# The corrections of clipped states in the mixer: a sorted list of places, worked four at a time, instead of a walk over all rows

## Chip, cores, metric

One core of a Trainium2 chip runs a whole model of four layers in one program. The metric is the device time of one execution in microseconds. The kernel before took 3464.84 us (median of 3 runs, 3463.93 to 3465.86).

## The reference, cut to what matters

The first half of layer 0 is a mixer over 4 sequences of 1024 steps with 128 channels. It widens the 128 channels to 256 and runs 16 states for each of them, forward and backward in time:

```
h0 = 0
step:  h = clip(h * A + x_t * Bm, -10, 10)      # A, Bm: 256 x 16
       y = sum over the 16 states of h * C      # C: 256 x 16
out = (forward + backward) * 0.5 * silu(gate);  result = out @ out_proj_w
```

A is -clip(exp(A_log), -10, -0.01), and because exp(A_log) is positive that is 0.01 for every state. Without the clipping, each state is therefore its Bm times one common scan of x. The clipping matters only where that product leaves the range -10 to 10. A top-2 mixture of 8 experts (128 to 256 to 128) over the same tokens follows in the same stage, and six more parts of the model after it.

## The kernel before, in words

All that the change touches is in `mixer_and_top2`, the first stage. Channels lie on the 128 partitions. A row k (0 to 3) is one of two directions times one of two channel tiles, and `S[k]` is its plain scan over 1024 steps, with 32 zero columns ahead of it (`LEAD`), since a correction begins 32 steps early. For sequence b, VectorE does this, in the order that its program writes out at the end of the function:

- `scan` (L618) makes S for the four rows. `reaches` (L622 to L624) takes the largest |S| of every 256 steps (`CHUNK`) and multiplies it by |B| of every state: 128 x 256 numbers (4 rows, 4 places, 16 states).
- `gains` writes G, the output as if no state were clipped. `take_masks` (L634 to L649) compares `most` with 9.99 on one partition and leaves, for each (row, state), the number and the place of 256-step pieces in which a state can be clipped: a mask of those with one such piece, a mask of those with several, and the places.
- `corrections` walks the masks twice, first those with one piece, then those with several (`many`). A walk is a loop over the 4 rows; each pass loads the row's mask into a register (L675), tests each group of four states, and in a group that has any, each state. A state that is set is worked by `correct` (L595 to L611): it loads the place into a register, writes 2 x 288 limits (L605, L606), scans 576 elements (L608), and adds 256 of the results to G (L611). Both arms of every test add the same numbers to the semaphore `fix`, so `gated` (L688 on) can wait for a constant.
- `gated` writes y = (G forward + G backward) * gate (L692, L693). TensorE's output product of the sequence (L312) waits for y; everything of that sequence's experts comes behind it.

The order over the sequences: for sequence 0 nothing is there to lie beside the corrections. For sequences 1 to 3, TensorE, ScalarE and GpSimd run the experts of the sequence before; TensorE's program has `output(p)` at a fixed place among them (turn 9 of 35, `MIXED`), and GpSimd's has `largest(p + 2)` at turn 20 (`REACH`), between products `weigh` (L560) for which TensorE's L352 waits. VectorE's `route` and `normalise` for the sequence before are ahead of `take_masks` in its own order.

Of the kernel before, what the change touches and what calls it, by code (L numbers as in the profile page):

```python
# [143 lines left out]
def mixer_and_top2(nc, X, XN, XT, ident, x_dram, in_proj_w, A_log, B_mat, C_mat, out_proj_w, ln_w, ln_b, gate_w, gate_b, w1, b1, w2, b2):  # L144
# [13 lines left out]
    QUAD = 4  # L158
# [6 lines left out]
    LEAD, CHUNK = 32, 256  # L165
    NCHUNK = SEQ // CHUNK
    WINDOW, ROW = LEAD + CHUNK, LEAD + SEQ
    LAG = 3
# [19 lines left out]
    with Stage(nc, "mix") as s:  # L188
# [5 lines left out]
        limS, nCBS = (s.sb(n, [P, NSEG, DS]) for n in ("limS", "nCBS"))  # L194
# [6 lines left out]
        S = s.sb("S", [P, NSEG, ROW])  # L201
        G = s.sb("G", [P, NSEG, SEQ])
        S_flat, G_flat = S[:].rearrange("p k t -> p (k t)"), G[:].rearrange("p k t -> p (k t)")
# [3 lines left out]
        bit = s.sb("bit", [1, NSEG, DS])  # L207
        place = s.sb("place", [1, NSEG, NCHUNK, DS])
        flags, placed = (s.sb(n, [1, NSEG, NCHUNK, DS]) for n in ("flags", "placed"))
        count, place_f, one, many = (s.sb(n, [1, NSEG, DS]) for n in ("count", "place_f", "one", "many"))  # L210
        mask_f = s.sb("mask_f", [1, 2, NSEG])
        masks = s.sb("masks", [1, 2, NSEG], mybir.dt.int32)
        places = s.sb("places", [1, NSEG * DS], mybir.dt.int32)
# [26 lines left out]
        fix = [s.sem(f"fix{b}") for b in range(BATCH)]  # L240
# [11 lines left out]
        with nc.Block() as block:  # L252
# [299 lines left out]
            def _(pool):  # L552
# [18 lines left out]

                largest(0)
# [14 lines left out]
            def _(dve):  # L587
# [3 lines left out]
                def correct(b, k, d, many):  # L591
                    n = k * DS + d
                    done = (many * NSEG * DS + n) * 3
                    if many:
                        steps, lead = SEQ, 0  # L595
                        sk = S_flat[:, bass.ds(k * ROW + LEAD, SEQ)]
                        gk = G_flat[:, bass.ds(k * SEQ, SEQ)]
                    else:
                        steps, lead = WINDOW, LEAD
                        at = dve.value_load(places[0:1, bass.ds(n, 1)], min_val=0, max_val=SEQ - CHUNK)  # L600
                        sk = S_flat[:, bass.ds(k * ROW + at, WINDOW)]
                        gk = G_flat[:, bass.ds(k * SEQ + at, CHUNK)]
                    L = limS[:].rearrange("p k d -> p (k d)")[:, bass.ds(n, 1)]
                    w = nCBS[:].rearrange("p k d -> p (k d)")[:, bass.ds(n, 1)]
                    ts(d1[:, 0:steps, 0], sk, -1.0, L, ALU.mult, ALU.add)  # L605
                    ts(d1[:, 0:steps, 1], sk, L, None, ALU.add).then_inc(fix[b], 1)  # L606
                    dve.wait_ge(fix[b], done + 1)
                    nc.vector.tensor_tensor_scan(q[:, 0:steps].rearrange("p t a -> p (t a)"), d0[:, 0:steps].rearrange("p t a -> p (t a)"),  # L608
                                                 d1[:, 0:steps].rearrange("p t a -> p (t a)"), 0.0, ALU.mult, ALU.min).then_inc(fix[b], 1)
                    dve.wait_ge(fix[b], done + 2)  # L610
                    stt(gk, q[:, lead:steps, 1], w, gk, ALU.mult, ALU.add).then_inc(fix[b], 1)  # L611
# [16 lines left out]
                def gains(b):  # L628
                    for k in range(NSEG):
                        c.link(ts(G[:, k], S[:, k, LEAD:], gain[:, k % CT:k % CT + 1], None, ALU.mult))  # L630

                def take_masks(b):
                    dve.wait_ge(most_ready, b + 1)
                    c.link(ts(flags[:], most[0:1].rearrange("p (s c d) -> p s c d", c=NCHUNK, d=DS), BOUND * 0.999, None, ALU.is_gt))  # L634
                    tt(placed[:], flags[:], place[:], ALU.mult).then_inc(ch, 1)
# [2581 lines left out]
```

## Time and profile before

| | |
|---|---|
| three runs | 3463.93, 3465.86, 3464.84 us |
| the profiled execution | 3498.89 us, span 3497.2 us, mean granted clock 0.883 |
| TensorE busy | 79% |
| VectorE busy | 54% |
| ScalarE, GpSimd busy | 40%, 27% |
| mixer stage with the top-2 experts | 0 to about 570 us |
| sequence 0: VectorE from the end of its list to y | 46.9 to 186.9 us |

Durations are of the profiled execution, which is 34 us longer than the median of the runs. "Idle before" in brackets is the time the engine sat idle ahead of an instruction, with what ended it; "issue" means that it waited for nothing the profile shows, and "DVEq" is VectorE's own sequencer, which for these lines is the register work and branches of the walk. Register, branch and semaphore instructions are not counted as busy and have no rows.

### The profile page before, as it was taken

The page shows a single profiled execution, that of the slowest core. Times are in us where ns is not written, and L with a number is a line of the kernel's source. Part 1 is how long each engine was busy: PE and PEld are TensorE (multiplying, and loading weights), DVE is VectorE, ACT ScalarE, POOL GpSimd, SP SyncE. Part 2 cuts the span into 40 slices and gives each one's busy share as a digit, 9 for nine tenths or more (in the row PEclk, how much of TensorE's full clock was granted, in tenths as well). Part 3 has the DMA queues.
Part 4 walks back from the last instruction along what each step waited for, and adds up shares of the span by engine and source line. Part 5 has one row for each costly group of instructions (what it writes and reads, how often), then busy time and mean ns, then how long its engine had stood idle before and what let it go on. Part 6 is the DMA issues. An engine that isn't in the chain of part 4 may idle for free. (4 is left out here: it accounts for less than half of the span.)

```text
span 3497.2 us, 32456 instructions
## 1 busy us (share of the span) xinstructions
PE 2779.8 (79%) x10134; PEld 1389.7 (40%) x10146; DVE 1899.3 (54%) x3672; ACT 1407.3 (40%) x2163; POOL 936.7 (27%) x606
## 2 busy tenths in 40 slices
PE   2047888999999979999978777595799999659517
PEld 1023444555555544444444443243233333137503
DVE  6546532222222276656455458312777777489786
ACT  1023433111111146666644421133477877526403
POOL 0014563000000000000033320303499999600005
PEclk6568999999999989999968888897899999779658
DMA  2011121000000066665500012011000000100001
GB/s 54 0 31 40 49 58 37 0 0 0 0 0 0 0 146 145 144 140 141 120 5 1 0 43 57 31 43 51 25 1 1 10 1 1 33 2 1 1 0 31
DMA packets 107458, 126.08 MB, mean 36 GB/s; under 512 B 22283, under 2 KB 60300, under 8 KB 107052
## 3 DMA queue, kind: packets, MB, share of 16 engines
q1 hardware_dynamic: 105260, 120.13, 14.1%
q0 software_dynamic: 2048, 4.20, 0.4%
q8 instruction: 64, 1.05, 0.1%
q14 instruction: 86, 0.70, 0.1%
HBM read 108.55 MB, written 14.16 MB: 35 GB/s over the span
## 5 line engine op out<-in xcount | busy, mean ns | idle before, releaser
L2432 PE MATMUL dots_x<-all_xt,delta_wE 128*128 128x512 f32 x768 | 366.2, 613 | 3.7 <-DVE dots_g L2527 2.3
L2417 POOL TENSOR_TENSOR dots_pr<-dots_g 128x512 f32<-128x512 f32 (+2 forms) x96 | 305.6, 3204 | 56.1 <-DVE dots_g L2527 48.2
L971 DVE SCALAR_TENSOR_TENSOR attn_sim<-attn_sc,attn_mask 128x512 f32<-128x512 f32 (+3 forms) x256 | 125.8, 491 | 316.9 <-PE attn_sc L897 313.8
L897 PE MATMUL attn_sc<-attn_q,attn_xb 128*128 128x512 f32 (+3 forms) x768 | 295.0, 486 | 0.0
L908 PE MATMUL attn_op<-attn_sim,attn_v 128*128 128x512 f32 (+3 forms) x768 | 295.0, 486 | 0.0
L1257 DVE TENSOR_TENSOR grp_h<-grp_sq,grp_cb 128x512 f32<-128x512 f32 x256 | 176.7, 692 | 191.1 <-ACT grp_sq L1145 170.7
L1085 PE MATMUL grp_po<-grp_h,grp_down 128*128 128x512 f32 x512 | 266.1, 602 | 6.1 <-DVE grp_h L1257 6.1
L1077 PE MATMUL grp_ph<-all_xt,grp_up 128*128 128x512 f32 x512 | 264.0, 598 | 0.5 <-ACT grp_sg L1161 0.5
L2524 DVE TENSOR_TENSOR dots_m<-dots_x,dots_sg 128x512 f32<-128x512 f32 x256 | 173.9, 689 | 137.3 <-PE dots_x L2432 131.1
L1139 ACT ACTIVATE grp_r<-grp_ph 128x512 f32<-128x512 f32 x272 | 162.4, 597 | 185.4 <-PE grp_ph L1077 183.7
L2432 PEld LDWEIGHTS dots_x<-all_xt,delta_wE 128*128 128x128 f32 x768 | 135.9, 190 | 234.8 <-issue 139.3
L560 POOL TENSOR_TENSOR mix_h<-mix_r,mix_cb 128x512 f32<-128x512 f32 x128 | 172.1, 1352 | 151.3 <-ACT mix_r L474 117.2
L2417 POOL TENSOR_TENSOR all_xn<-dots_g 128x1536 f32<-128x1536 f32 (+2 forms) x64 | 205.2, 3223 | 11.0 <-DVE dots_g L2527 5.6
L897 PEld LDWEIGHTS attn_sc<-attn_q,attn_xb 128*128 128x128 f32 x768 | 141.0, 190 | 125.7 <-issue 107.1
L908 PEld LDWEIGHTS attn_op<-attn_sim,attn_v 128*128 128x128 f32 x768 | 141.0, 190 | 98.4 <-issue 68.9
L2527 DVE SCALAR_TENSOR_TENSOR dots_g<-dots_m,dots_x 128x512 f32<-128x512 f32 x256 | 163.1, 679 | 0.0
L946 ACT ACTIVATE attn_sim<-attn_sc 128x512 f32<-128x512 f32 x128 | 76.4, 597 | 205.6 <-PE attn_sc L897 205.6
L1145 ACT ACTIVATE grp_sq<-grp_r 128x512 f32<-128x512 f32 x256 | 159.1, 621 | 0.0
L474 ACT ACTIVATE mix_r<-mix_ph,mix_b1s 128x512 f32<-128x512 f32 x128 | 87.9, 687 | 160.2 <-PE mix_ph L344 137.1
L1085 PEld LDWEIGHTS grp_po<-grp_h,grp_down 128*128 128x128 f32 x512 | 94.6, 191 | 138.7 <-issue 95.9
L352 PE MATMUL mix_acc<-mix_h,mix_w2s 128*128 128x512 f32 x256 | 132.2, 606 | 20.4 <-POOL mix_h L560 20.4
L312 PE MATMUL mix_po<-mix_woT,mix_y 128*128 128x128 f32 x128 | 20.1, 331 | 157.8 <-DVE mix_y L693 157.8
(622 smaller groups left out, 4947.2 us busy)
## 6 DMA issues: line engine op xcount, KB each, us to landing
grp_cb<-grp_combine SPq DMA_DIRECT2D x512, 128.0 KB, 3.3
mix_cb<-top_weights SPq DMA_DIRECT2D x64, 256.0 KB, 3.2
cap_xs<-cap_zero SPq DMA_DIRECT2D x7, 320.0 KB, 5.0
experts_xe<-cap_xs SPq DMA_DIRECT2D x7, 320.0 KB, 3.2
all_x<-in_L_attn_x_dram SPq DMA_DIRECT2D x4, 512.0 KB, 5.3
cap_w<-in_L_ffn_W_dram SPq DMA_DIRECT2D x1, 2048.0 KB, 8.9
cap_ys<-experts_yo SPq DMA_DIRECT2D x8, 256.0 KB, 2.3
delta_h<-all_xn SPq DMA_DIRECT2D x1, 2048.0 KB
```

Of the source, the lines that this page charges most:

```text
L560: nc.gpsimd.tensor_tensor(h[:, J % HB], r[:, J % RB], cb[:, n % CB], ALU.mult).then_inc(h_ready, 1)
L897: nc.tensor.matmul(sc[k % SC][:, 0:w], xb[:, m * P:(m + 1) * P], q[:, par, n0:n0 + w], start=True, stop=True).then_inc(s_mm, 1)
L908: ins = nc.tensor.matmul(op[half][:, n0 - half * GROUP:n0 - half * GROUP + w], v[:, par, m], sim[:, par, k, 0:w], start=False, stop=False)
L1077: nc.tensor.matmul(ph[J % 2][:], w, XT[:, g * GROUP:(g + 1) * GROUP], start=True, stop=True).then_inc(up_mm, 1)
L1085: nc.tensor.matmul(po[g % 2][:], w, h[:, J % HB], start=(j == 0), stop=(j == NJ - 1)).then_inc(down_mm, 1)
L1139: nc.scalar.activation(r[:, J % RB], ph[J % 2][:], ACT.Relu).then_inc(relu_done, 1)
L1145: nc.scalar.activation(sq[:, J % RB], r[:, J % RB], ACT.Square).then_inc(sq_done, 1)
L1257: tt(h[:, J % HB], sq[:, J % RB], cb[:, n % CB], ALU.mult).then_inc(h_done, 1)
L2417: nc.gpsimd.tensor_tensor(slot[w % SLOTS][:, at:at + n], a_, b_, ALU.mult).then_inc(pool_ready, 1)
L2432: nc.tensor.matmul(bank(n, sh)[:], wE[:, 1 - k % 2, a, sh], XTj[:, k // 2, par::2], start=True, stop=True).then_inc(u_mm, 1)
L2524: tt(m[:, n % 2, sh - 1], bank(n, sh)[:], sg[:, n % 2], ALU.mult).then_inc(m_ready, 1)
L2527: ins = stt(g[:, I % 2, sh - 1, k], m[:, n % 2, sh - 1], 0.0, bank(n, 0)[:], ALU.max, ALU.mult)
```

## The change

Places are 128 steps long instead of 256, so a window is 160 columns and `reach` and `most` have 512 columns instead of 256. `take_masks` makes one number for every (row, state) that has just one place: `found` holds the place, `first_code` the row and the state, and together they are column * 128 + (row * 16 + state + 1). Eight rounds of top-eight and replace sort the 64 numbers in descending order. What has several places goes into masks as before, with their sum ahead of them. `corrections` goes over 4 parties of 16 entries of the sorted list. Where the first of a party is not zero, it works four times four entries: four register loads, then for each entry the addition of the result of the group before (`add_pending`) and its two limit instructions, and at the end one scan over 4 x 160 x 2 elements. Empty entries within a party work on a limit of 1 and a weight of 0. The last four results are added after the loop. The walk over rows with several places is behind one test of the sum. G gets rows of 1056 columns, so that one offset serves S and G. GpSimd makes the constant tables. In all:

```diff
-    LEAD, CHUNK = 32, 256
+    LEAD, CHUNK = 32, 128
+    ENTRIES = NSEG * DS
+    RADIX = 128
+    STEP = CHUNK * RADIX
+    SINGLE, SEVERAL = NCHUNK * STEP, 2 * NCHUNK * STEP
...
     (GpSimd, before largest(0))
+                for c_ in range(NCHUNK):
+                    nc.gpsimd.memset(place[:, :, c_], float(SINGLE + c_ * STEP))
+                for d in range(DS):
+                    nc.gpsimd.memset(bit[:, :, d:d + 1], float(1 << d))
+                    for k in range(NSEG):
+                        last = nc.gpsimd.memset(first_code[:, k, d:d + 1], float(k * ROW * RADIX + k * DS + d + 1))
+                last.then_inc(tables, 1)
+                nc.gpsimd.memset(q[:, 2 * CT * C // 2:SEQ // 2], 0.0).then_inc(tables, 1)
...
+                def none_pending():
+                    for i in range(QUAD):
+                        dve.reg_mov(last_at[i], 0)
+                        dve.reg_mov(last_col[i], 0)
+
+                def add_pending(b, i):
+                    at = dve.snap(last_at[i], min_val=0, max_val=(NSEG - 1) * ROW + SEQ - CHUNK)
+                    col = dve.snap(last_col[i], min_val=0, max_val=ENTRIES)
+                    gk = G_flat[:, bass.ds(at, CHUNK)]
+                    stt(gk, q[:, i * WINDOW + LEAD:(i + 1) * WINDOW, 1], nCBS[:, bass.ds(col, 1)], gk, ALU.mult, ALU.add).then_inc(bounded[b], 1)
+
+                def correct_four(b, n):
+                    code = [dve.value_load(codes[0:1, bass.ds(n * QUAD + i, 1)], min_val=0, max_val=LAST_CODE) for i in range(QUAD)]
+                    dve.wait_ge(traced[b], n + 1)
+                    for i in range(QUAD):
+                        if i:
+                            dve.wait_ge(bounded[b], n * (QUAD + 1) + i)
+                        add_pending(b, i)
+                        at, col = code[i] >> 7, code[i] & (RADIX - 1)
+                        dve.reg_mov(last_at[i], at)
+                        dve.reg_mov(last_col[i], col)
+                        sk, L = S_flat[:, bass.ds(at, WINDOW)], limS[:, bass.ds(col, 1)]
+                        ts(d1[:, i * WINDOW:(i + 1) * WINDOW, 0], sk, -1.0, L, ALU.mult, ALU.add)
+                        last = ts(d1[:, i * WINDOW:(i + 1) * WINDOW, 1], sk, L, None, ALU.add)
+                    last.then_inc(bounded[b], 1)
+                    dve.wait_ge(bounded[b], (n + 1) * (QUAD + 1))
+                    nc.vector.tensor_tensor_scan(q[:, 0:QUAD * WINDOW] ..., d0[:, 0:QUAD * WINDOW] ...,
+                                                 d1[:, 0:QUAD * WINDOW] ..., 0.0, ALU.mult, ALU.min).then_inc(traced[b], 1)
...
     (correct becomes correct_row: the same four instructions over 1024 steps, for rows with several places)
...
                 def take_masks(b):
                     dve.wait_ge(most_ready, b + 1)
-                    (thresholds, count, places, two masks: 10 instructions)
+                    c.link(stt(flags[:], most[0:1] ..., BOUND * 0.999, place[:], ALU.is_gt, ALU.mult))
+                    c.link(redu(total[:], flags[:].rearrange("p s c d -> p s d c"), AX.X, ALU.add))
+                    (several, found; mask_f, begin; mask_f sum, left: three pairs on 1 x 64; masks)
+                    for i in range(ENTRIES // EIGHT):
+                        top = listed[:, i * EIGHT:(i + 1) * EIGHT]
+                        c.link(nc.vector.max(top, left[:, i % 2]))
+                        if i + 1 < ENTRIES // EIGHT:
+                            c.link(nc.vector.match_replace(left[:, (i + 1) % 2], top, left[:, i % 2], 0.0))
+                    c.link(ts(listed[:], listed[:], float(SINGLE), 0.0, ALU.subtract, ALU.max))
+                    c.link(nc.vector.tensor_copy(codes[:], listed[:]))
...
                 def corrections(b):
                     dve.sem_inc(apart, 1)
-                    for many in range(2):
+                    dve.sem_inc(traced[b], 1)
+                    none_pending()
+                    with dve.Fori(0, ENTRIES // PARTY) as party:
+                        leader = dve.value_load(codes[0:1, bass.ds(party * PARTY, 1)], min_val=0, max_val=LAST_CODE)
+                        with dve.If(leader > 0):
+                            with dve.Fori(0, PARTY // QUAD) as four:
+                                correct_four(b, party * (PARTY // QUAD) + four)
+                            dve.sem_inc(apart, 1)
+                        with dve.Else():
+                            dve.sem_inc(traced[b], PARTY // QUAD)
+                            dve.sem_inc(bounded[b], (QUAD + 1) * (PARTY // QUAD))
+                    dve.wait_ge(traced[b], ENTRIES // QUAD + 1)
+                    for i in range(QUAD):
+                        add_pending(b, i)
+                        dve.wait_ge(bounded[b], ENTRIES // QUAD * (QUAD + 1) + i + 1)
+                    any_row = dve.value_load(masks[0:1, 0:1], min_val=0, max_val=NSEG * (2 ** DS - 1))
+                    with dve.If(any_row > 0):
                         with dve.Fori(0, NSEG) as k:
                             (as before, with correct_row)
+                    with dve.Else():
+                        dve.sem_inc(fix[b], 3 * ENTRIES)
```

## Rows read from the trace of the kernel before

**Rows 1.** Stages: window, length, busy of five engines with instructions, granted clock, DMA share, GB/s.
```profile
47.00:187.00 140.00, 6.51 (x8) 2.44 (x8) 70.03 (x113) 2.65 (x5) 0.00 (x0) 0.51 0.00 0
```

**Rows 2.** Waits of TensorE, 185 to 560 us: who for whom, total, times, longest.
```profile
PE mix_po L312 <- DVE mix_y L693: 157.8, 3, 138.0
PE mix_acc L352 <- POOL mix_h L560: 20.4, 2, 10.3
```

**Rows 3.** Timeline of VectorE, list making of sequence 0: start, duration, instruction, idle before.
```profile
44.17 0.27 DVE L634 TENSOR_SCALAR mix_flags<-mix_most 1x256 f32<-1x256 f32 x1
...
44.82 0.56 DVE L636 TENSOR_REDUCE mix_count<-mix_flags 1x64 f32<-1x256 f32 x1
...
46.75 0.16 DVE L649 CAST mix_masks<-mix_mask_f 1x8 int32<-1x8 f32 x1
49.48 0.37 DVE L605 TENSOR_SCALAR mix_d<-mix_S,mix_limS 128x288 f32 x1 [2.56 <-issue]
```

**Rows 4.** Timeline of VectorE, corrections of sequence 0 and one scan after.
```profile
79.08 0.37 DVE L605 TENSOR_SCALAR mix_d<-mix_S,mix_limS 128x288 f32 x1 [1.22 <-issue]
...
82.70 0.37 DVE L605 TENSOR_SCALAR mix_d<-mix_S,mix_limS 128x288 f32 x1 [0.85 <-issue]
...
95.56 0.37 DVE L605 TENSOR_SCALAR mix_d<-mix_S,mix_limS 128x288 f32 x1 [2.38 <-issue]
...
186.88 1.22 DVE L692 TENSOR_TENSOR mix_y<-mix_G 128x1024 f32<-128x1024 f32 x1 [13.00 <-DVEq L686]
...
202.36 2.29 DVE L618 TENSOR_TENSOR_SCAN mix_S<-mix_decay,mix_xs 128x1024 f32<-128x1024 f32 x1
```

**Rows 5.** Groups by line, 0 to 700 us: a correction's instructions; busy, mean ns.
```profile
L608 DVE TENSOR_TENSOR_SCAN mix_q<-mix_d 128x576 f32<-128x576 f32 x28 | 38.0, 1358 | 1.0
...
L611 DVE SCALAR_TENSOR_TENSOR mix_G<-mix_q,mix_nCBS,mix_G 128x256 f32 x28 | 13.6, 485 | 6.7 <-DVE mix_q L608 6.7
...
L605 DVE TENSOR_SCALAR mix_d<-mix_S,mix_limS 128x288 f32 x28 | 10.4, 371 | 49.3 <-issue 49.3
```

**Rows 6.** Groups by line, whole run: VectorE's top-eight and replace instructions.
```profile
L3057 DVE MATCH_REPLACE8 sink_left<-sink_best,sink_left 32x1024 f32<-32x1024 f32 x15 | 17.9, 1196 | 0.0
...
L1224 DVE MAX8 grp_top<-grp_v 128x8 f32<-128x64 f32 x32 | 4.8, 213 | 0.0
...
L3057 DVE MATCH_VALUE_LOAD sink_left<-sink_best,sink_left 32x8 f32 x15 | 1.2, 79 | 0.5
```

**Rows 7.** Timeline of VectorE: first instruction behind the walks of sequences 1, 2, 3.
```profile
264.30 1.23 DVE L692 TENSOR_TENSOR mix_y<-mix_G 128x1024 f32<-128x1024 f32 x1 [28.76 <-DVEq L686]
...
349.65 1.22 DVE L692 TENSOR_TENSOR mix_y<-mix_G 128x1024 f32<-128x1024 f32 x1 [19.52 <-DVEq L686]
...
437.97 1.34 DVE L692 TENSOR_TENSOR mix_y<-mix_G 128x1024 f32<-128x1024 f32 x1 [29.16 <-DVEq L686]
```

**Rows 8.** Timeline of GpSimd around its all-reduces.
```profile
41.63 1.20 POOL L570 PARTITION_ALL_REDUCE mix_most<-mix_reach  x1 [39.83 <-issue]
215.03 1.06 POOL L570 PARTITION_ALL_REDUCE mix_most<-mix_reach  x1 [172.20 <-DVE mix_reach L624]
...
312.92 1.08 POOL L570 PARTITION_ALL_REDUCE mix_most<-mix_reach  x1 [6.01 <-issue]
321.12 4.92 POOL L560 TENSOR_TENSOR mix_h<-mix_r,mix_cb 128x512 f32<-128x512 f32 x4 [7.12 <-issue]
```

**Rows 9.** Timeline of TensorE: output products of sequences 1, 2, 3.
```profile
269.35 6.51 PE L312 MATMUL mix_po<-mix_woT,mix_y 128*128 128x128 f32 x32 [17.67 <-DVE mix_y L693]
...
360.00 3.73 PE L312 MATMUL mix_po<-mix_woT,mix_y 128*128 128x128 f32 x32
...
445.98 3.84 PE L312 MATMUL mix_po<-mix_woT,mix_y 128*128 128x128 f32 x32 [2.14 <-DVE mix_y L693]
```

**Rows 10.** DMA queues, 60 to 173 us: packets, MB, share of the 16 engines.
```profile
q14 instruction: 1, 0.01, 0.0%
```

**Rows 11.** The same, 235.6 to 264.3 us.
```profile
q14 instruction: 5, 0.04, 0.4%
```

More of the change, by code:

```diff
@@ L206, in mixer_and_top2 @@
         most = s.sb("most", [P, NSEG * NCHUNK * DS])
[L207 to L213, printed above, removed]
+        bit, first_code, several = (s.sb(n, [1, NSEG, DS]) for n in ("bit", "first_code", "several"))
+        place, flags = (s.sb(n, [1, NSEG, NCHUNK, DS]) for n in ("place", "flags"))
+        total, found, begin = (s.sb(n, [1, NSEG, DS]) for n in ("total", "found", "begin"))
+        left = s.sb("left", [1, 2, ENTRIES])
+        listed = s.sb("listed", [1, ENTRIES])
+        mask_f = s.sb("mask_f", [1, 1 + NSEG])
+        masks = s.sb("masks", [1, 1 + NSEG], mybir.dt.int32)
+        codes = s.sb("codes", [1, ENTRIES], mybir.dt.int32)
         gw = s.sb("gw", [P, E])
@@ L239, in mixer_and_top2 @@
             "reach_ready", "most_ready", "out_mm", "x_added", "vector_chain", "apart"))
-        fix = [s.sem(f"fix{b}") for b in range(BATCH)]
+        fix, bounded, traced = ([s.sem(f"{n}{b}") for b in range(BATCH)] for n in ("fix", "bounded", "traced"))
+        tables = s.sem("tables")
         gates_in, w1_in, w2_in, stats_done, var_ready, std_ready, xn_ready = (s.sem(n) for n in (
@@ L589, in _ @@
                 tt, ts, stt, redu = nc.vector.tensor_tensor, nc.vector.tensor_scalar, nc.vector.scalar_tensor_tensor, nc.vector.tensor_reduce
-                def correct(b, k, d, many):
-                    n = k * DS + d
[L593 to L606, printed above, removed]
+                last_at = [nc.alloc_register(mybir.EngineType.DVE, f"last_at{i}") for i in range(QUAD)]
@@ new lines, in _ @@
+                last_col = [nc.alloc_register(mybir.EngineType.DVE, f"last_col{i}") for i in range(QUAD)]
+                def none_pending():
[7 more added lines that the diff above has]
+                    stt(gk, q[:, i * WINDOW + LEAD:(i + 1) * WINDOW, 1], nCBS[:, bass.ds(col, 1)], gk, ALU.mult, ALU.add).then_inc(bounded[b], 1)
@@ L629, in gains @@
                     for k in range(NSEG):
-                        c.link(ts(G[:, k], S[:, k, LEAD:], gain[:, k % CT:k % CT + 1], None, ALU.mult))
+                        c.link(ts(G[:, k, 0:SEQ], S[:, k, LEAD:], gain[:, k % CT:k % CT + 1], None, ALU.mult))
                 def take_masks(b):
                     dve.wait_ge(most_ready, b + 1)
-                    c.link(ts(flags[:], most[0:1].rearrange("p (s c d) -> p s c d", c=NCHUNK, d=DS), BOUND * 0.999, None, ALU.is_gt))
-                    tt(placed[:], flags[:], place[:], ALU.mult).then_inc(ch, 1)
@@ L636, in take_masks @@
-                    redu(count[:], flags[:].rearrange("p s c d -> p s d c"), AX.X, ALU.add).then_inc(ch, 1)
+                    if b == 0:
+                        dve.wait_ge(tables, 2)
+                    c.link(stt(flags[:], most[0:1].rearrange("p (s c d) -> p s c d", c=NCHUNK, d=DS), BOUND * 0.999, place[:], ALU.is_gt, ALU.mult))
+                    c.link(redu(total[:], flags[:].rearrange("p s c d -> p s d c"), AX.X, ALU.add))
+                    stt(several[:], total[:], float(SEVERAL), bit[:], ALU.is_ge, ALU.mult).then_inc(ch, 1)
@@ L640, in take_masks @@
[L640 to L642 removed]
+                    redu(mask_f[:, 0:1], mask_f[:, 1:], AX.X, ALU.add).then_inc(ch, 1)
+                    tt(left[:, 0].rearrange("p (s d) -> p s d", d=DS), found[:], begin[:], ALU.add).then_inc(ch, 1)
+                    c.n += 2
                     dve.wait_ge(ch, c.base + c.n)
[L644 removed]
@@ L746, in _ @@
                 c.link(nc.vector.memset(S[:, :, 0:LEAD], 0.0))
-                for c_ in range(NCHUNK):
-                    last = nc.vector.memset(place[:, :, c_], float(c_ * CHUNK))
-                c.link(last)
                 c.link(stt(nCB[:], Cm[:], -0.5, B[:], ALU.mult, ALU.mult))
```

63 lines of the change are left out of this document (36 added, 27 removed).

## The prediction

> **What bounds the kernel now.** I read the 40 slices of the page first: TensorE is at 70 to 100% nearly everywhere, but at 20, 0 and 40% in the first three slices of 87 us. The stage table shows why: in the 140 us from 47 to 187 us TensorE works 6.5 us at a granted clock of 0.51, GpSimd not at all, and VectorE 70 us [rows 1]. TensorE's waits name it: of 157.8 us waited for the mixer's y, 138.0 are one wait, that of sequence 0 [rows 2]. All of VectorE's corrections lie on the path there. The timeline of VectorE then shows that all 28 corrections of the run belong to sequence 0 [rows 5], and that the walks of sequences 1 to 3 find nothing and still take 28.8, 19.5 and 29.2 us [rows 7]. The third is as long as the first; the second is shorter because its sequencer had run ahead while VectorE was held up in the instructions before. Of these, TensorE waits 17.7 us for sequence 1, nothing for sequence 2 and 2.1 us for sequence 3 [rows 9].
>
> **What the data ask for.** I computed the plain scans and reaches from the reference's inputs: 28 (row, state) pairs of sequence 0 pass 9.99, as in the trace, and none of the other sequences. Each of the 28 lies in a single piece, with 256 and with 128 steps alike. So the new list has 28 entries: two parties run, eight groups of four with four blank entries in the last, and the walk over rows is skipped in all four sequences.
>
> **What a register instruction costs.** Within a group of states, the next state follows after 0.85 us idle if it is set and 1.22 us if one is skipped [rows 4]. A skip is four sequencer instructions, so 0.092 us each. Between the addition and the next limits are eight sequencer instructions with one load: 0.85 + 0.485 for the addition that they run beside [rows 5], so 1.34 us, less seven of 0.092: a load from SBUF is about 0.6; I take 0.55. An empty pass of 22 is then 21 x 0.092 + 0.55 = 2.5 us; the second walk of sequence 0 took 13.00 us for four [rows 4], 3 us more. Eight are 20 us against 28.8 [rows 7], 9 more, with five packets of instruction code in that stretch [rows 11], so a missing block of code costs some 1.8 us (the queue is shared by several engines: an estimate).
>
> **Part 1, the corrections of sequence 0.** Before: from the end of the list, 46.9 [rows 3], to 186.88 [rows 4], 140.0 us: four instructions of 0.37, 0.37, 1.36 and 0.485 a correction [rows 5], about 2.77 with their overlap, x 28 = 78, the rest sequencer.
> After, one group of four. VectorE: elements cost 1.02 ns (top-eight of 64 in 0.213, replace of 1024 in 1.196 [rows 6]), so the limits take 0.371 - 0.131 = 0.24 and the addition 0.35; the scan's slope is (2.29 - 1.36) / 448 = 2.08 ns [rows 4, 5], so 1280 elements take 2.82. Sum 8 x 0.24 + 4 x 0.35 + 2.82 = 6.1 us. Sequencer: I count 4 x 4 instructions for the loads, 4 x 13 for the entries (two snapped registers with their checks, addresses, waits on register values, shift and mask), five for scan and loop: 73 with 4 loads, 69 x 0.092 + 4 x 0.55 = 8.5 us. The loads, 3.3 us, can run while the previous scan is at work; the rest, 5.2, covers limits and additions, and at its end the last limits and the start of the scan cost 0.2 more: 8.7 us. No row shows a load beside a long scan. Bounds: VectorE alone, 6.1, and nothing beside anything, 8.5 + 6.1 = 14.6. The nearest rows, where sequencer work does run beside the addition, speak for the middle; I take 8.7. Eight groups: 70 us (49 to 117).
> Around them: 12 instructions ahead (1.1), four passes of the party loop (ten with a load, 1.4 us each, 5.6), the tail of four additions each waited for (36 instructions, 3.3, plus 0.5), the test with its load (1.1), three missing blocks of code (5.4; the jump over the 250 instructions of the row walk is one): 17 us. Together 87 against 140.0: -53. What it hides: nothing else was running, so the whole of it counts, and what is late next at y is VectorE itself.
>
> **Part 2, making the list.** Before: 44.17 to 46.9, 2.7 us [rows 3]. After: the first instruction 0.485 + 0.26 = 0.75 over 512 columns, the reduction 0.56 + 0.26 = 0.82 [rows 3, 5], five short steps on 64 columns 1.3, eight top-eights at 0.213 + 0.04 for the chained wait, seven replaces at 0.079 + 0.21 + 0.04 [rows 6], two at the end 0.45: 7.6 us, +4.9. The reach takes 0.3 more. On the path for sequences 0 and 1.
> The all-reduce has twice the columns. For sequence 0 the library load is behind the wait for reach, so it is at work from 41.63 [rows 8] and done by 44.17, where VectorE goes on without waiting [rows 3]: 1.2 to 2.5 us, which doubled ends at 44.0 to 46.7. I put 1 us on it (0 to 2.5).
> Sequence 0 so far: -53 + 4.9 + 0.3 + 1 = -46.8.
>
> **Part 3, sequences 1 to 3.** The empty walk becomes 12 + 4 x 10 + 36 + 7 = 95 instructions with 5 loads, 11.0 us, + 0.5 for additions that can't hide, + three missing blocks 5.4: 17 us (11 to 22). Sequence 1: -11.8 + 5.2 = -6.6, of the 17.67 us that TensorE waits [rows 9]; all of it counts. Sequence 2: TensorE came to its product without a wait [rows 9], since the four instructions that make y, from 349.65 on [rows 7] and 1.2 to 2.2 us each, had ended 3.5 us before; the walk's gain (2.5) less 5.2 eats 2.7 of these: 0. Sequence 3: y comes 7 us earlier, of which 2.1 count [rows 9].
> The all-reduces of sequences 2 and 3 sit in GpSimd's queue between products: 6.0 + 1.1 + 7.1 = 14 us each from product to product, with TensorE waiting 10.3 and 10.1 [rows 2, 8]. Each grows by 1.1 (its recorded length) to 2.2 us, and TensorE waits for it: +3.3. The 89 small memsets on GpSimd and the one of 128 x 256 x 2 lie in its idle 39.8 us at the start [rows 8]; uncovered they would cost at most some 9 us. VectorE's own memsets that go (0.6 us) lay ahead of a wait for ScalarE.
> Sum: -46.8 - 6.6 - 2.1 + 3.3 = -52 us: 3498.9 to 3447 for the profiled execution. The median of the runs is 34 us below; nothing in the stage depends on what makes that difference, so 3464.8 - 52 = 3413.
>
> **A page weighed.** In 113 us of sequence 0's loop, with its 302 instructions, one packet of code came [rows 10]; in the 29 us of a first pass over new code, five [rows 11]. The Trainium skill (Runtime: NRT & Kernel Launch, Instruction fetch mechanics) says that a taken branch whose target isn't in the current two pages of 256 instructions forces a fetch. By that rule a body of 302 could be fetched anew with each of four passes, which rows 10 don't show; the new inner body, some 75, would stay. The rule speaks for the jump over the row walk, priced above as a missing block.
>
> **Rivals.**
> A. Register loads wait until VectorE is idle, so nothing lies beside the scan: 11.5 us a group, +22: 3435. For: the 1.34 us above also fit a load that waited for the addition. Chance 0.17.
> B. Register work is cheaper than counted, several operations being packed into one instruction, and a group takes 7 us: -14, and 2 less for each walk: 3397. For: the packing is seen in the kernel before. Chance 0.15.
> C. The walks of sequences 1 to 3 don't shrink, because jumps over code make new misses (28 us stay): sequence 1 costs +5.2 instead of -6.6, sequence 3 +3 instead of -2.1, sequence 2 +1.7: 3432. Against: 95 instructions in place of 176. Chance 0.1.
> D. Slower than before: each pass of the loop over four fetches its code anew, because the body, the party's head and the walk behind them share blocks. From 15.2 us a group on, the change loses: 14.6 with nothing overlapped and one fetch of 1.8 is 16.4, x 8 = 131 against 70: +61, 3474. Against: rows 10. Chance 0.03.
> E. It doesn't do what it says: a single entry counted as several places opens the row walk. Four passes of 3.25 us, and limits, scan and addition over 1024 steps at the slopes above, 8.9 us: +22, 3435. Against: the inputs. Chance 0.02.
> The forecast keeps 0.53.
>
> **How the numbers follow.** Predicted 3413. A range of 3388 to 3440 takes in the forecast with a group at 7.5 to 10, rivals A, C and E, and the near part of B; outside are the far part of B and D. Of this kernel 0.2% (7 us) is about what can be told from no change. Faster: all but D and what lies near it, 0.96; within 0.2%: 0.01; slower 0.03.
>
> **What would show it.** In the new profile: y of sequence 0 at 137 to 142 us; eight scans of 128 x 1280 of 2.8 us each, spaced 8.7 us (11.5: A; 7: B; over 15: D); 7.6 us from the first instruction of the list to its end; a gap behind the walks of sequence 1 of 17 us or less (28: C); TensorE's wait for y of sequence 0 near 91 us and of sequence 1 near 11, none for 3; GpSimd's pauses at the all-reduces 15 to 16 us. No scan of 2048 elements (E). The forecast is wrong if the scans' spacing is off by more than 3 us, or if TensorE's wait for sequence 0 shrinks and a later wait, for y of 2 or for GpSimd, grows by as much.

## The result, and the profile after

The changed kernel takes 3381.47 us (median of 4 runs, 3380.22 to 3382.33) against 3465.35 us for the kernel before on the same chip: a ratio of 0.9759, 95% interval 0.9744 to 0.9773, or -84 us. The forecast was -52, in the range 3388 to 3440. The direction was right, the size was not.

The profiled execution of the changed kernel took 3380.9 us. The one of before took 3498.9 us, 34 us more than the runs. Later runs of the kernel before, on three chips, took 3497 to 3498 us on two of them and 3462 us on the third, so this profile most likely comes from a chip of the slower kind. The two kinds differ by some 36 us in one place, between the first write of the capacity routing's zeroed tables (2106.3 in the profile of before, 2026.0 after) and the first sums of the delta rule (2502.0 and 2385.2): 395.7 against 359.2 us. That stretch is the same code, and its length goes with the chip and not with the kernel: it is 394 to 397 us in all nine profiles of the slower kind, seven of them of other kernels than before, and 359 to 360 us in all five of the faster. Everything below is about the mixer stage, which ends with the first weight copy of the attention behind it: 590.8 us before, 512.2 after, -78.6 us. Second profiles of the two kernels have 593.7 and 513.4, so a difference of stages is known to some 3 us.

The stage that was nearly empty is about half as long. The stage table of the changed kernel (columns as in [rows 1]) shows its first 69 us, with VectorE busy for 53 of them; y begins 3.6 us later, so that like for like, from 47 us to y, it is 72.6 us in place of 139.9:

```profile
47.00:116.00 69.00, 6.68 (x12) 2.57 (x10) 53.03 (x140) 3.17 (x5) 0.00 (x0) 0.52 0.00 0
```

TensorE's waits in the changed kernel, 110 to 480 us, answer to [rows 2]: 138.0 has become 70.1, only one other wait for y is left (2.0 us), and there is a new row, 7.3 us for the normalised input of sequence 2.

```profile
PE mix_po L320 <- DVE mix_y L764: 72.1, 2, 70.1
PE mix_acc L360 <- POOL mix_h L568: 22.7, 5, 11.3
...
PE mix_tr L329 <- DVE all_xn L718: 7.3, 1, 7.3
```

The timeline of VectorE in sequence 0 answers to [rows 3, 4]: first and last instruction of the list, start of the first group, scans of the first groups, the passage from the first party to the second (81.72 to 86.75), the last scan, the first addition of the tail and the first instruction of y.

```profile
45.44 0.67 DVE L676 SCALAR_TENSOR_TENSOR mix_flags<-mix_most,mix_place 1x512 f32<-1x512 f32 x1
...
52.78 0.18 DVE L698 CAST mix_codes<-mix_listed 1x64 int32<-1x64 f32 x1
58.31 0.35 DVE L619 SCALAR_TENSOR_TENSOR mix_G<-mix_q,mix_nCBS,mix_G 128x128 f32 x1 [5.35 <-issue]
...
61.42 2.83 DVE L636 TENSOR_TENSOR_SCAN mix_q<-mix_d 128x1280 f32<-128x1280 f32 x1
65.15 0.35 DVE L619 SCALAR_TENSOR_TENSOR mix_G<-mix_q,mix_nCBS,mix_G 128x128 f32 x1 [0.90 <-DVE mix_q L636]
...
68.23 2.83 DVE L636 TENSOR_TENSOR_SCAN mix_q<-mix_d 128x1280 f32<-128x1280 f32 x1
...
81.72 2.83 DVE L636 TENSOR_TENSOR_SCAN mix_q<-mix_d 128x1280 f32<-128x1280 f32 x1
86.75 0.35 DVE L619 SCALAR_TENSOR_TENSOR mix_G<-mix_q,mix_nCBS,mix_G 128x128 f32 x1 [2.21 <-issue]
...
110.05 2.83 DVE L636 TENSOR_TENSOR_SCAN mix_q<-mix_d 128x1280 f32<-128x1280 f32 x1
114.01 0.35 DVE L619 SCALAR_TENSOR_TENSOR mix_G<-mix_q,mix_nCBS,mix_G 128x128 f32 x1 [1.13 <-DVEq L732]
...
119.64 1.23 DVE L763 TENSOR_TENSOR mix_y<-mix_G 128x1024 f32<-128x1024 f32 x1 [3.71 <-DVEq L757]
```

The list takes 7.5 us, 45.44 to 52.96. The scans start 6.8 us apart, once 8.1 where the party changes. Between a scan's end (64.25) and the next addition (65.15) there are 0.90 us, in the later groups 0.82 to 0.84.

Sequence 1 in the same timeline, for [rows 7]: the last instruction ahead of the walk ends at 173.47. The first of the four blank additions is at 177.78 and y begins at 184.11. The empty walk with its additions takes 10.6 us, where it took 28.8.

```profile
177.78 0.35 DVE L619 SCALAR_TENSOR_TENSOR mix_G<-mix_q,mix_nCBS,mix_G 128x128 f32 x1 [4.31 <-DVEq L732]
...
184.11 1.22 DVE L763 TENSOR_TENSOR mix_y<-mix_G 128x1024 f32<-128x1024 f32 x1 [3.65 <-DVEq L757]
```

The code packets in that stretch (the queue view, columns as in [rows 11]), two where there were five:

```profile
q14 instruction: 2, 0.02, 0.4%
```

TensorE's timeline, for [rows 9]: the output products of sequences 0 to 3, and the turning of the normalised input ahead of the second.

```profile
124.70 5.59 PE L320 MATMUL mix_po<-mix_woT,mix_y 128*128 128x128 f32 x32 [70.06 <-DVE mix_y L764]
...
172.59 1.08 PE L329 MATMUL mix_tr<-all_ident,all_xn 128*128 128x128 f32 x4 [7.34 <-DVE all_xn L718]
...
192.01 5.47 PE L320 MATMUL mix_po<-mix_woT,mix_y 128*128 128x128 f32 x32 [2.00 <-DVE mix_y L764]
...
281.93 3.73 PE L320 MATMUL mix_po<-mix_woT,mix_y 128*128 128x128 f32 x32
...
367.97 3.73 PE L320 MATMUL mix_po<-mix_woT,mix_y 128*128 128x128 f32 x32
```

GpSimd's timeline, for [rows 8]: the all-reduce with 512 columns is recorded with 1.80 us instead of 1.08, and the two pauses between products go from 14.2 and 14.0 us to 14.8 and 15.2.

```profile
234.36 1.80 POOL L578 PARTITION_ALL_REDUCE mix_most<-mix_reach  x1 [5.84 <-issue]
243.28 4.92 POOL L568 TENSOR_TENSOR mix_h<-mix_r,mix_cb 128x512 f32<-128x512 f32 x4 [7.12 <-issue]
```

From these rows comes the ledger of the stage:

| stretch | before | after | change | forecast |
|---|---|---|---|---|
| to the first output product | 191.9 | 124.7 | -67.2 | -46.8 |
| first to second | 77.4 | 67.3 | -10.1 | -6.6 |
| second to third | 90.7 | 89.9 | -0.7 | +1.65 |
| third to fourth | 86.0 | 86.0 | +0.1 | -0.45 |
| fourth to the attention | 144.8 | 144.2 | -0.6 | 0 |

### The profile page after: what moved, and what is told of

Its sections match the earlier page's. It is cut to its first block and busy times, and to the rows that moved or that the text cites. A ratio compares the mean times of both kernels' runs of the same rounds, so it can differ in the third digit from the quotient of the medians.

```text
span 3379.1 us, 32162 instructions
## 1 busy us (share of the span) xinstructions
PE 2774.0 (82%) x10146; PEld 1388.3 (41%) x10146; DVE 1909.5 (57%) x3754; ACT 1408.2 (42%) x2163; POOL 946.8 (28%) x695
## 3 DMA queue, kind: packets, MB, share of 16 engines
q0 software_dynamic: 2048, 4.20, 0.4%
## 5 line engine op out<-in xcount | busy, mean ns | idle before, releaser
L2484 POOL TENSOR_TENSOR all_xn<-dots_g 128x1536 f32<-128x1536 f32 (+2 forms) x64 | 205.2, 3224 | 10.9 <-DVE dots_g L2594 5.7
L360 PE MATMUL mix_acc<-mix_h,mix_w2s 128*128 128x512 f32 x256 | 132.0, 605 | 22.8 <-POOL mix_h L568 22.7
```

Of the source, the lines that this page charges most:

```text
L2484: nc.gpsimd.tensor_tensor(slot[w % SLOTS][:, at:at + n], a_, b_, ALU.mult).then_inc(pool_ready, 1)
```

## The experiments

Each is compared by its ratio to the kernel before on the same chip. The experiments ran in three sets on three chips: before_again, before_test, rows_always and one_a_scan on the first, the loads and the signals on the second, the rest on the third. There the kernel before takes 3498, 3498 and 3462 us. Gains in us across sets are made from ratios, or from where the attention begins in the trace. In the timelines a scan's row has its start first: the spacing of two is the time of a group of four.

### before_again: the kernel before, profiled again

> The kernel before, profiled a second time. The profile of before was 34 us longer than its runs, that of after is not. If the 34 us were a disturbance of that one execution, this profile is about 3466 us, with the mixer stage again 587.6 us to the first instruction of the attention that follows, and the 20 us more of before between the zeroing of the capacity tables (2106) and the selection matrices of the delta rule (2408) gone. If they belong to the kernel, they are there again.

3497.11 us, ratio 0.9996 (0.9986 to 1.0007). The attention begins at 593.7 us, and the stretch in the capacity routing is within 2 us as long as in the first profile: 2108.1 to 2502.0. The 34 us belong to the chip, not to one disturbed execution: the runs of the kernel before beside it take as long. Both alternatives that I had written were off in that they looked to the kernel or the execution.

### before_test: the test alone

```diff
+                    (in take_masks: a sum over the second mask and its cast, two small instructions)
                     walk(0)
+                    any_row = dve.value_load(any_i[0:1, 0:1], ...)
+                    with dve.If(any_row > 0):
                         walk(1)
+                    with dve.Else():
+                        dve.sem_inc(fix[b], 3 * NSEG * DS)
```

> The kernel before with the walk over states with several places behind one test of the sum of its mask, nothing else. Theory (each empty pass of a walk costs 2.5 to 3.3 us of sequencer time): the second walk of sequence 0 goes from 13.0 us to about 3.5, and those of sequences 1 to 3 lose 9 us each. On the path are 9 us of sequence 0 and 9 of the 17.7 that TensorE waits for sequence 1, and 2 for sequence 3: -20 us, 3445. Rival (the code jumped over costs new misses that eat the gain): no more than -8 us.

3475.97 us against 3498.29, ratio 0.9944 (0.9927 to 0.9960): -22 us, as the theory said. The walk that was 13.0 us [rows 4] is 4.0, the walks of sequence 1, 28.8, are 19.0:

```profile
179.61 1.23 DVE L705 TENSOR_TENSOR mix_y<-mix_G 128x1024 f32<-128x1024 f32 x1 [3.99 <-DVEq L699]
...
246.92 1.23 DVE L705 TENSOR_TENSOR mix_y<-mix_G 128x1024 f32<-128x1024 f32 x1 [18.97 <-DVEq L699]
```

A quarter of the whole gain is this one branch.

### rows_always: everything but the test

```diff
-                    any_row = dve.value_load(masks[0:1, 0:1], ...)
-                    with dve.If(any_row > 0):
                         with dve.Fori(0, NSEG) as k:
                             ...
-                    with dve.Else():
-                        dve.sem_inc(fix[b], 3 * ENTRIES)
```

> The changed kernel without the test: the walk over rows with several places runs in each sequence and finds nothing. Theory (four empty passes cost 13 us, as in sequence 0 of the kernel before): +10 us on the path of sequence 0, +10 for sequence 1, some of the next two: +20 to +25 us, 3404. Rival (with so little else in the loop the code stays and a pass is cheap, below 2 us): +6 to +10 us.

Ratio 0.9841 (0.9825 to 0.9858), against 0.9772 for the changed kernel: 0.69% of 3498, +24 us, as expected; by the traces the attention begins 19 to 20 us later (532.6 against 512.2 and 513.4). The end of the walk is 10.9 us in sequence 0 in place of 3.7, and 12.6 in sequence 1 in place of 3.65:

```profile
126.49 1.23 DVE L757 TENSOR_TENSOR mix_y<-mix_G 128x1024 f32<-128x1024 f32 x1 [10.86 <-DVEq L751]
...
200.30 1.23 DVE L757 TENSOR_TENSOR mix_y<-mix_G 128x1024 f32<-128x1024 f32 x1 [12.62 <-DVEq L751]
```

Taking the test away from the new kernel costs about what adding it to the old one gave.

### one_a_scan: the list, but one entry at a time

```diff
-                            with dve.Fori(0, PARTY // QUAD) as four:
-                                correct_four(b, party * (PARTY // QUAD) + four)
+                            with dve.Fori(0, PARTY) as one:
+                                correct_one(b, party * PARTY + one)   # load, 2 limits, scan of 320, addition
```

> The changed kernel with its list, but every entry of a running party worked alone: one load, two limits, one scan of 320 elements, one addition, each waited for; 32 passes instead of 8. Theory (what was gained by four at once is that the loads and register work of four lie beside one scan, and one chain of waits instead of four): an entry costs about 0.55 + 11 x 0.09 + 0.22 + 0.83 + 0.35 + 0.5 of waits, 3.2 us, 32 of them 102 us instead of 54.6: +48 us, 3429. Rival (the gain came from the list's straight loop in place of tests, and four at once adds little): under +20 us.

Ratio 0.9874 (0.9858 to 0.9891): 3450.84 us, -44 against the kernel before and +36 against the changed one (1.02%) by the ratios. The trace shows less: y of sequence 0 is 34.6 us later than in the changed kernel (154.3 against 119.6), and at the attention 27 to 28 us are left (540.2). An entry takes 2.87 us:

```profile
61.13 0.30 DVE L643 TENSOR_SCALAR mix_d<-mix_S,mix_limS 128x160 f32 x1 [1.02 <-issue]
61.35 0.30 DVE L644 TENSOR_SCALAR mix_d<-mix_S,mix_limS 128x160 f32 x1
61.68 0.82 DVE L646 TENSOR_TENSOR_SCAN mix_q<-mix_d 128x320 f32<-128x320 f32 x1
62.64 0.35 DVE L650 SCALAR_TENSOR_TENSOR mix_G<-mix_q,mix_nCBS,mix_G 128x128 f32 x1
64.00 0.30 DVE L643 TENSOR_SCALAR mix_d<-mix_S,mix_limS 128x160 f32 x1 [1.01 <-issue]
```

Before, a correction took 4.5 us (127 us for 28), with the same kind of register load ahead of each. Of that fall to 2.87, [rows 4] show the two parts: where two set states adjoin, 3.62 us lie between their first limits (79.08 to 82.70), so about 0.9 us went with the tests and skips; the other 0.75 us are about what the shorter window saves in the scan (1.36 to 0.82), the addition (0.49 to 0.35) and the limits (0.37 to 0.30 each). Four at once makes it 1.7 us an entry. The direction of the theory was right, at 28 to 36 us instead of 48, and the rival (under 20) is out. Its 3.2 us for an entry were too high.

### loads_behind and one_load: do the loads run beside the scan?

```diff
+                    dve.wait_ge(traced[b], n + 1)       # loads_behind: the wait first
+                    dve.sem_inc(apart, 1)
                     code = [dve.value_load(...) for i in range(QUAD)]
-                    dve.wait_ge(traced[b], n + 1)
```

> The changed kernel with the wait for the previous scan ahead of the four register loads instead of behind them; one signal more. Theory A (the loads run beside the scan, as the kernel has them): a group of four grows from 6.75 us by the 2.8 us of the scan, to 9.6, +22 us in all. Theory B (loads from SBUF wait for VectorE to be idle anyway, rival A of the forecast): the spacing stays within 0.3 us.

Ratio 0.9818 (0.979 to 0.9847), 16 us more than the changed kernel by ratio and by y of sequence 0 (135.6 against 119.6), where 22 were expected. The spacing is 9.1 us in place of 6.75, so the loads do run beside the scan. Rival A of the forecast is out. The trace of the changed kernel shows it directly: it holds the sequencer's instructions too, which the views leave out, and beside the scan of 68.23 to 71.06 four register loads are recorded at 68.89, 69.63, 70.34 and 71.05.

```profile
62.08 2.82 DVE L637 TENSOR_TENSOR_SCAN mix_q<-mix_d 128x1280 f32<-128x1280 f32 x1
...
71.19 2.83 DVE L637 TENSOR_TENSOR_SCAN mix_q<-mix_d 128x1280 f32<-128x1280 f32 x1
```

```diff
-                    code = [dve.value_load(codes[0:1, bass.ds(n * QUAD + i, 1)], ...) for i in range(QUAD)]
+                    code = [dve.value_load(codes[0:1, bass.ds(n * QUAD, 1)], ...)] * QUAD    # one_load
```

> The changed kernel with one register load for each group of four, its entry worked four times (part of the corrections is left out); 34 instructions in the loop instead of 52. If the 0.84 us between a scan's end and the next addition are the tail of loads that outlast the scan (16 instructions with 4 loads, 3.6 us against 2.8), the gap falls to about 0.2 and a group to 6.1 us, -5 us in all. If the gap is the latency of the wait for the scan, it stays at 0.84 and a group at 6.7.

Ratio 0.974 (0.971 to 0.977), an interval that overlaps that of the changed kernel. The trace is clearer: the spacing falls to 6.0 us, the gap between a scan's end and the next addition from 0.84 to 0.18, as expected. It stops there though 34 instructions are only some 3.6 us at the forecast's prices: VectorE's own work, 6.1 in the forecast, is the floor.

```profile
65.52 2.82 DVE L636 TENSOR_TENSOR_SCAN mix_q<-mix_d 128x1280 f32<-128x1280 f32 x1
...
71.55 2.82 DVE L636 TENSOR_TENSOR_SCAN mix_q<-mix_d 128x1280 f32<-128x1280 f32 x1
```

### signals_beside and signals_among: is the loop bound by the sequencer?

```diff
                     code = [...]
+                    for i in range(8): dve.sem_inc(apart, 1)        # signals_beside
                     dve.wait_ge(traced[b], n + 1)
...
                         last = ts(...)
+                        (3, 3, 2 signals behind the first three entries)   # signals_among
```

> The changed kernel with eight signals more for each group, behind the loads and ahead of the wait for the scan. If the loads outlast the scan (sequencer-bound there), each signal adds its 0.09 us: +0.74 a group, 7.5, +6 us. If the sequencer has time to spare beside the scan: nothing.

> The changed kernel with eight signals more for each group, among the entries (3, 3, 2 behind the limits of the first three). If the entries' 0.7 us each are sequencer time (7 instructions at 0.09): +0.74 a group, +6 us. If they are VectorE's time (0.22 + 0.22 + 0.28 us of issue) with the sequencer ahead: under +0.3 a group. Together with the signals beside the scan: both grow by 0.74 if the whole loop is bound by the sequencer.

Both spacings grow, to 7.57 and 7.62 us: 0.10 to 0.11 a signal, at either place. (The runs, with ratios of 0.9791 and 0.9798 and intervals of 0.976 to 0.9827 together, don't tell them from the changed kernel.) That doesn't make the whole loop bound by the sequencer. From a scan's start to the first addition the changed kernel takes 3.66 us (68.23 to 71.89), in which the sequencer goes through 20 instructions without a pause, and the scan ends 0.8 us before them: there it is the bound. From the first addition to the next scan it takes 3.09 us, and one_load, with fewer register instructions there, 3.02 (68.53 to 71.55): there VectorE's pace and the sequencer's are level, so that more work for the sequencer costs time and less gives next to none. In signals_among the compiled loop has 60 instructions instead of 52, in signals_beside 59. The two fences are the first kernel's and the second's.

```profile
69.83 2.82 DVE L638 TENSOR_TENSOR_SCAN mix_q<-mix_d 128x1280 f32<-128x1280 f32 x1
...
77.40 2.82 DVE L638 TENSOR_TENSOR_SCAN mix_q<-mix_d 128x1280 f32<-128x1280 f32 x1
```

```profile
70.86 2.82 DVE L639 TENSOR_TENSOR_SCAN mix_q<-mix_d 128x1280 f32<-128x1280 f32 x1
...
78.48 2.83 DVE L639 TENSOR_TENSOR_SCAN mix_q<-mix_d 128x1280 f32<-128x1280 f32 x1
```

### lead8 and no_bounds: less for VectorE, less for the sequencer

```diff
-    LEAD, CHUNK = 32, 128
+    LEAD, CHUNK = 8, 128                       # lead8
...
-  dve.value_load(codes[...], min_val=0, max_val=LAST_CODE)
+  nc.s_assert_within(dve.value_load(codes[...]), ..., skip_runtime_bounds_check_because=...)   # no_bounds
```

> The changed kernel with windows that begin 8 steps early instead of 32 (the decay is 0.01, so 8 steps forget everything): the scan has 1088 elements instead of 1280 and the limits 136 instead of 160, VectorE's work for a group falls by 0.40 + 0.20 us. If the loop is bound by the sequencer (52 instructions, 4 of them loads, 6.75 us), the spacing of the scans stays within 0.1 us and the time within 2 us. If it is bound by VectorE and the latency of its waits, the spacing falls to 6.2 us and the time by 5.

3383.55 us against 3383.09 for the changed kernel beside it (ratios 0.9776 and 0.9772): no difference. VectorE's scan is 0.4 us shorter and the spacing is 6.73. The limits hardly got shorter: 0.28 to 0.29 us for 136 columns against 0.30 for 160, so the 0.20 us a group that the expectation took off for them weren't there to gain:

```profile
67.67 2.43 DVE L636 TENSOR_TENSOR_SCAN mix_q<-mix_d 128x1088 f32<-128x1088 f32 x1
...
74.40 2.42 DVE L636 TENSOR_TENSOR_SCAN mix_q<-mix_d 128x1088 f32<-128x1088 f32 x1
```

> The changed kernel without the bounds check behind each of the four loads of a group: 44 instructions in the loop instead of 52. Bound by the sequencer: 8 x 0.092 less, 6.0 us a group, where VectorE's own 6.1 takes over as bound: -5 us. Bound by VectorE: under 1 us.

3376.27 us, ratio 0.9754 (0.974 to 0.9768); the interval overlaps that of the changed kernel, but the spacing is plain: 6.08 us with eight instructions fewer, down to VectorE's floor. TensorE's long wait is 61.0 us instead of 69.9. Of these 9 us some 6.5 lie ahead of the last scan (103.51 against 110.05). Another 2.3 have nothing to do with the checks' own time: the branch over the row walk, with one packet of instruction code right behind it in the changed kernel, takes 2.85 us there and 0.59 us here. The edit moved the code; why the branch is cheap here no run shows.

```profile
66.37 2.82 DVE L637 TENSOR_TENSOR_SCAN mix_q<-mix_d 128x1280 f32<-128x1280 f32 x1
...
72.45 2.82 DVE L637 TENSOR_TENSOR_SCAN mix_q<-mix_d 128x1280 f32<-128x1280 f32 x1
```

These two are the cleanest pair: beside the scan, taking work from VectorE gives nothing, and taking instructions from its sequencer shortens the group until VectorE's own time is reached.

### after_again and all_in

> The changed kernel again, timed and profiled beside the kernel before on the chip of the other experiments, where the kernel before takes 3498 us instead of 3465. If the mixer stage alone accounts for the gain, the first instruction of the attention is at 512 as before and the kernel is 78 to 84 us faster, 3415 to 3420; the 34 us by which both chips differ lie behind the attention, in the routing and the delta rule.

3383.09 us, ratio 0.9772 (0.9759 to 0.9786), attention at 513.4 us. It ran on a chip where the kernel before takes 3462 us, not on the kind I had expected, so it repeats the first comparison. The stretch from the attention to the last stage's experts is 2832 to 2840 us for all kernels on the chips of the first two sets and in the first profile of before, and 2801 to 2802 us for the changed kernel and its variants on the faster kind; the change doesn't touch it.

```diff
+    LEAD 8; no bounds checks; normalise_in(b + 1) ahead of take_masks(b)
+                    any_place = dve.value_load(any_i[0:1, 0:1], min_val=0, max_val=1)
+                    with dve.If(any_place > 0):
                         (sorting, parties, tail, row walk)
+                    with dve.Else():
+                        dve.sem_inc(ch, 17); dve.sem_inc(fix[b], 3 * ENTRIES)
```

> A version meant to beat both: windows 8 steps early, no bounds checks in the group's loop, the sorting and all of the corrections behind one test whether any place is in the list at all, and the normalising of the next input ahead of the list. Sequence 0: a group at 5.6 to 5.9 us, -7 to -9, +1.3 for the test. Sequence 1: list 5 us shorter and walk 7 us shorter, TensorE's wait for the normalised input 7.3 down to 2.9, its wait for y 2.0 gone: -6. Sequence 2 and 3 nothing. In all -12 to -15 us against the changed kernel. Rival (the jump over the 370 instructions costs a miss that eats what it saves): -7.

3370.67 us (3369.72 to 3373.8), ratio 0.9740 (0.9727 to 0.9753): 12 us below the changed kernel on the same chip, and the fastest of all. The groups are 5.7 us apart. Behind the test, sequence 1 has 8.9 us to y (three packets of code in it), where sorting and walk took 5.1 and 10.6. Of the 8.9 us one branch, that over the sorting and the corrections, takes 7.4; so the miss that the rival expected is there and eats part of the gain:

```profile
73.12 2.42 DVE L639 TENSOR_TENSOR_SCAN mix_q<-mix_d 128x1088 f32<-128x1088 f32 x1
...
78.80 2.42 DVE L639 TENSOR_TENSOR_SCAN mix_q<-mix_d 128x1088 f32<-128x1088 f32 x1
...
162.99 0.14 DVE L697 CAST mix_any_i<-mix_any_f 1x1 int32<-1x1 f32 x1
172.00 1.23 DVE L779 TENSOR_TENSOR mix_y<-mix_G 128x1024 f32<-128x1024 f32 x1 [8.87 <-DVEq L773]
```

TensorE's wait for the normalised input is gone (2.9 us were expected to stay) and part of it has come back as a wait for y, 4.1 us instead of 2.0 (expected: none). Four things were changed at once here, so no single one of them is shown to give its share.

## Why the prediction was off

**What held.** The bound was right: VectorE's corrections of sequence 0, with nothing beside them. So were the 28 entries, the eight scans, the skipped row walk (no scan of 2048 elements is in the trace), the list at 7.5 us for 7.6, its start 1.3 us later, the scan at 2.83 us for 2.82, the addition at 0.35, VectorE's 6.1 us for a group (6.0 in one_load), and the loads beside the scan. A limit was put at 0.24 us; it is recorded with 0.30, but the next instruction starts 0.22 us after it, which comes to the same sum.

**The step that failed** is in part 1: "Sequencer: I count 4 x 4 instructions for the loads, 4 x 13 for the entries ... 73 with 4 loads". The compiled loop has 52. The term that was mis-sized is "the rest, 5.2", with the 0.2 behind it: from the first addition to the next scan 3.09 us were measured, 2.3 less. The loads with the end of the loop came to 3.66 us where 3.3 stood. Together that is 6.75 us a group for 8.7. This is rival B, which had 0.15. Eight groups cost 55 us instead of 70: 15 of the 26.6 us that the forecast missed in the stage.

**The prices were right only in the mean.** With the forecast's own, 48 x 0.092 + 4 x 0.55 = 6.6 us for the 52 instructions; 6.75 was measured. But the readings behind them were off. The trace of before has three sequencer instructions for a skipped state (77.59 to 77.96), not four, so 0.12 us each; and 1.34 less seven of 0.092 is 0.69 for a load, not 0.6. What the traces record from one sequencer instruction's start to the next's is uneven: 0.07 to 0.08 us for plain arithmetic, 0.10 for a semaphore, 0.08 for a branch not taken and 0.19 to 0.30 for one taken, 0.34 for a load, 0.10 to 0.26 for one that computes several results. An empty pass of the old walk is 18 instructions in 2.68 us (181.64 to 184.32), where the forecast had 22 in 2.5.

**Around the groups and in the empty walk.** The same miscount: the tail has 8 instructions, not 36, the test 4, not 7, and an empty walk 60 instead of 95. Beside it stands a second term that came out smaller, the missing blocks of code: 5.4 us were put for three of them in either sequence, while one branch was long in each, that over the row walk, with 2.85 and 2.80 us. So sequence 1 took 10.6 us instead of 17 (the first 2 us of its register work lay beside the instructions before), and in sequence 0 everything but the groups 12 us instead of 17, another 5 us, about half of it by the count and half by the code blocks.

**Sequence 1** gave -10.1 instead of -6.6. TensorE's wait for y fell by 15.7 us, which is all but 2 of it, and 4.4 came back in a wait that I hadn't named: `take_masks` stands ahead of `normalise_in` in VectorE's order, so the longer list pushes TensorE's turning of the next input, 7.3 us of wait where it was 3.0. (The remaining 1.2 us between 15.7 and 10.1 are in no wait named here.) I had priced the longer list only on the way to y. In all_in, which moves `normalise_in` ahead, that wait is gone; the sorting was moved there too.

**GpSimd.** The pauses grew by 0.6 and 1.2 us, not 1.1 to 2.2 each. TensorE's waits for its products went from 20.4 to 22.7 us, +2.3 for a forecast of +3.3.

**The sum.** Stage: -78.6 measured, -52 forecast; the difference is 20.4 in sequence 0 (15 groups, 5 around them), 3.5 in sequence 1, 2.4 in sequence 2, and the rest within 1. The runs' -84 (79 to 89 by the interval) agrees with the stage alone, at the edge of the interval.

**The range** left out "the far part of B". B had been priced at 7 us a group with 2 less for each walk, 3397. Its own tail, test and walks share the count and would have made that some 4 us lower (an estimate: 31 instructions of tail and test and 35 of the empty walk at 0.092, less the 2 already taken), still inside the range. On top of B come the code blocks at about half of what was put for them, and 2.4 us in sequence 2. That makes 3387 by the stage's -78.6. The measured 3381.5 is another 5 us lower, no more than the interval of the comparison. The terms that share the count failed together, and no rival put them together with the blocks.

**The page weighed** gave no term of its own. A single packet of code came during the groups (60 to 113 us), in their first pass, and every later jump back to the head of the 52 instructions took some 0.3 us. The rule of the Trainium skill (Runtime: NRT & Kernel Launch, Instruction fetch mechanics) speaks of targets outside the two current pages. It fits the long branches over the row walk (2.85 and 2.80 us, with packets right behind them); that the same branch took 0.59 us in no_bounds shows that it can't be priced from the length of the jump alone.

## What to carry to other kernels

A loop with register loads, dynamic addresses and conditional arms is priced stretch by stretch between its waits, each by its sequencer instructions or by VectorE's own time, whichever is longer. For the first, 0.09 us each and 0.55 for a load from SBUF gave the loop of 52 within 0.2 us here, but an empty pass of 18, full of taken branches, 0.6 us too low. Count in the compiled program or the trace of like code, not in source lines, and if the count is uncertain, carry that through every term at once. A walk over flags that finds nothing isn't free: one test ahead of it gave 22 to 24 us here, with no change to the work. When a step ahead of another in an engine's order grows, look at what stands behind it on that engine, not only at the way to the result.

## What was not expected of the hardware

- Chips differ: the kernel before took 3462 to 3465 us on some and 3497 to 3498 us on others, with the difference in one stretch (359 against 396 us, the capacity routing; what in it differs is open). Absolute times of different sets can't be compared; ratios to the kernel beside can.
